# Rounding the encoder's angles on ScalarE instead of VectorE, in the first layer of a graph network

## The reference

```
rel_t     = node_vec[src] - edge_weight                        # one number per edge
rel_t_enc = cos(rel_t[:, None] * time_w + time_b)              # 32 numbers per edge
e         = concat([rel_t_enc, edge_attr_64]) @ We             # 96 -> 128
k, v      = (x @ Wk + bk)[src] + e, (x @ Wv + bv)[src] + e
alpha     = sum(q[dst] * k, per head) / 8
out       = segment_softmax(alpha, dst) weighted sum of v, by dst
x         = layernorm(x + out + x @ Wskip + bskip)
```

## Time and profile before

| | |
|---|---|
| median of 3 runs | 12685.32 us (12684.47 to 12685.91) |
| time of the profiled execution | 12758.32 us |
| its span | 12756.5 us |
| first and last gather of the first layer (L560) | 226.0 us and 6285.6 us |
| PE, DVE, ACT, POOL busy from 300 to 6000 us | 4130.52, 4032.91, 2634.28, 3696.79 us |
| the same from 6400 to 12756 us | 3715.91, 2565.70, 1396.91, 5152.92 us |

### The profile page before, as it was taken

How to read it: one execution, slowest core, us unless ns; L and a number is a source line. 1 busy time by engine, 2 the same in 40 slices (tenths; PEclk the granted TensorE clock), 3 DMA queues, 4 the chain that set the end, 5 groups by cost and what they waited for, 6 DMA issues and landing times.

```text
span 12756.5 us, 215589 instructions
## 1 busy us (share of the span) xinstructions
PE 8280.4 (65%) x44603; PEld 7400.1 (58%) x44604; DVE 7035.3 (55%) x23935; ACT 4268.4 (33%) x14084; POOL 9104.8 (71%) x7644
## 2 busy tenths in 40 slices
PE   5777777777777777777645555555555555555555
PEld 2666666666666666666635555555555555555555
DVE  4776776777777777767763333333333333333334
ACT  1444444444444444444422222222222222222221
POOL 2666666666666666666468888888888888888884
PEclk8777877787777777777766666666666666666667
DMA  6555555555555555555533333333333333333335
GB/s 184 150 149 146 148 149 149 148 152 148 150 148 148 150 152 150 148 149 149 135 37 35 35 35 35 35 35 35 35 35 35 35 35 35 35 35 35 35 35 120
DMA packets 1699357, 1205.64 MB, mean 95 GB/s; under 512 B 749995, under 2 KB 1471983, under 8 KB 1699023
## 3 DMA queue, kind: packets, MB, share of 16 engines
q0 software_dynamic: 634368, 675.42, 32.8%
q1 hardware_dynamic: 1013840, 503.68, 15.2%
q10 hardware_dynamic: 51072, 25.69, 0.7%
HBM read 924.83 MB, written 279.22 MB: 94 GB/s over the span
## 4 chain that ended last, share of the span: by engine, by line
DMA 22%; issue 20%; POOL 19%; DVE 13%; another core or an unknown queue 9%; PE 8%; DVEq 4%; SPq 3%; ACT 2%; POOLq 0%; ACTq 0%
DMA part_scratch<-kve,idx 21%; POOL part_scratch L609 19%; DVE y_all L1142 3%; PE bank L703 2%; DVE acc L1275 2%; PE bank L694 1%; DVEq L375 1%; PE bank L684 1%; DVEq L273 1%; PE bank L676 1%; DVE ohT L1135 1%; ACT wv L859 1%; DVE oh L1188 1%; DVE oh L1181 1%
## 5 line engine op out<-in xcount | busy, mean ns | idle before, releaser
L609 POOL DMA_INDIRECT part_scratch<-kve,idx x3232 | 5134.7, 1589 | 1056.8 <-issue 884.2
L560 POOL DMA_INDIRECT kv<-kv_scratch,took x3520 | 3544.5, 1007 | 2303.4 <-issue 1366.8
L761 PE MATMUL bank<-ident,kv 128*128 128x128 f32 x3232 | 753.4, 377 | 2403.8 <-DVE ohT L1364 2314.6
L1390 DVE TENSOR_TENSOR idx<-kv,twins 128x4 int32<-128x4 f32 x808 | 131.4, 163 | 3627.2 <-DMA part_scratch<-kve,idx 3627.2
L761 PEld LDWEIGHTS bank<-ident,kv 128*128 128x128 f32 x3232 | 489.4, 188 | 2582.1 <-ACT kv L940 2217.7
L859 ACT ACTIVATE wv<-tables,weights 128x65 f32<-128x65 f32 x7040 | 1771.5, 337 | 3.5 <-PE bank L703 2.5
L771 PE MATMUL bank<-ohT,oh 128*128 128x128 f32 x6464 | 1644.2, 435 | 148.6 <-DVE oh L1356 138.8
L771 PEld LDWEIGHTS bank<-ohT,oh 128*128 128x128 f32 x6464 | 1408.1, 321 | 423.7 <-DVE oh L1356 357.0
L947 ACT ACTIVATE oh<-bank 128x512 f32<-128x512 f32 x808 | 482.4, 597 | 3258.4 <-PE bank L771 3258.3
L703 PE MATMUL bank<-wv,oh 128*128 128x130 f32 x7040 | 1302.3, 342 | 363.4 <-issue 239.3
L1123 DVE TENSOR_TENSOR tables<-kv,bank 128x512 f32<-128x512 f32 x880 | 599.7, 681 | 1682.1 <-remote 1610.8
(11 more groups left out here) (166 smaller groups left out, 9952.4 us busy)
## 6 DMA issues: line engine op xcount, KB each, us to landing
kve<-nodes_scratch SPq DMA_DIRECT2D x880, 256.0 KB
feat<-in_edge_attr_dram SPq DMA_DIRECT2D x880, 96.0 KB
kv<-kv_scratch,took POOLq DMA_INDIRECT x3520
qb<-q_scratch SPq DMA_DIRECT2D x880, 64.0 KB
part_scratch<-kve,idx POOLq DMA_INDIRECT x3232
part_scratch<-zrow SPq DMA_DIRECT2D x220, 128.0 KB
feat<-in_edge_attr_dram SPq DMA_DIRECT2D x880, 32.0 KB
kv<-part_scratch ACTq DMA_DIRECT2D x56, 448.0 KB, 6.0
```

The lines of the kernel that those rows point to most:

```text
L560: pool.indirect_dma_start(kv[:, k, g, :], None, kv_d, bass.IndirectOffsetOnAxis(ap=took[:, j, g, 0:1].bitcast(I32), axis=0)).then_inc(s_ga ...
L609: pool.indirect_dma_start(part_d[g], bass.IndirectOffsetOnAxis(ap=idx[:, k, g:g + 1], axis=0), sum_ring[:, k, g, :], None, compute_op=ALU. ...
L761: op = pe.transpose(banks[0][:, g * P:(g + 1) * P], taken[:, st.k, 0, g:g + 1].to_broadcast([P, P]), ident[:, :])
```

## The change

DVE's `angle(1)` goes away. A new stage on ACT, `turn_stage`, adds MAGIC as the bias of an Identity activation, with the bias in a column `magic` of one element per partition, and signals `s_turn`. It stands directly ahead of `sine_stage` on ACT and waits for DVE's `angle(0)`. What was `angle(2)` is now `angle(1)`; it waits for `s_turn` and stands on DVE behind `ke_stage`. `ANG`, the number of angle steps on DVE for a batch, is 2 instead of 3. The column `magic` is set once at the start.

```diff
+        magic = sb("magic", [P, 1])
...
-        ANG = 3
+        ANG = 2
...
+            def turn_stage(st):
+                act.wait_ge(s_ang, ANG * st.batch() + 1)
+                act.activation(turns[:, :, :], encodings(st), ACT.Identity, bias=magic[:, :]).then_inc(s_turn, 1)
+
             def sine_stage(st):
                 act.wait_ge(s_ang, ANG * (st.batch() + 1))
...
-                    sines = [(sine_stage, 16)] if k % BATCH == 0 else []
+                    sines = [(turn_stage, 16), (sine_stage, 16)] if k % BATCH == 0 else []
...
+            dve.memset(magic[:, :], MAGIC)
...
+                    if n == 1:
+                        dve.wait_ge(s_turn, st.batch() + 1)
                     if n == 0:
                         op = dve.tensor_tensor(a, a, brow[:, :].unsqueeze(1).to_broadcast([P, BATCH * G, TD]), ALU.add)
-                    elif n == 1:
-                        wait(dve, s_ang, done)
-                        op = dve.tensor_scalar(t, a, MAGIC, None, ALU.add)
                     else:
                         op = dve.scalar_tensor_tensor(out=a, in0=t, scalar=MAGIC, in1=a, op0=ALU.subtract, op1=ALU.subtract)
...
-                    at(i, k, *turn[0], (ve_stage, 14), *turn[1], (ke_stage, 14), *turn[2], (block_stage, 0), *once(5, forward_stage),
+                    at(i, k, *turn[0], (ve_stage, 14), (ke_stage, 14), *turn[1], (block_stage, 0), *once(5, forward_stage),
```

More of the change, by code:

```diff
@@ L237, in build @@
         s_oh, s_oht, s_rel0, s_pen, s_gap = sem("s_oh"), sem("s_oht"), sem("s_rel0"), sem("s_pen"), sem("s_gap")
+        s_turn = sem("s_turn")
         s_rel, s_arg, s_ang, s_enc, s_feat, s_featc = sem("s_rel"), sem("s_arg"), sem("s_ang"), sem("s_enc"), sem("s_feat"), sem("s_featc")
```

## The result

| | before | after |
|---|---|---|
| median of 4 runs each | 12685.61 us (12684.47 to 12686.27) | 12915.60 us (12907.28 to 12924.54) |
| time of the profiled execution | 12758.32 us | 12924.54 us |
| its span | 12756.5 us | 12922.7 us |

The changed kernel takes 1.0182 times as long (95% interval 1.0164 to 1.0199): slower by 230 us, where 55 were forecast, and outside the range. The profiled executions differ by only 166 us, since the one of before lay 73 us above its median and the one of after 9 us above its own.

A forecast was written before the change was run, and what follows sets the result against it. No engine was full; a loop of POOL's eight gathers and angle multiplication, then DVE's odd-step additions, bounds it. Per round 0.4 + 0.3 - 0.2 = 0.5 us, times 110 = +55 us: about 12740 us, range 12640 to 12870.

The forecast's parts named there:

- the mechanism of the wait, and the side: DVE's last angle step waits for ACT's turn, partly covered by idleness: slower, 0.42 as likeliest case, 0.58 for slower overall.
- ACT's own price: ACT, 440 added Identity activations over 128x256 with a bias column: 0.50 us each, ends 0.34 and 0.71.
- table load ahead of the turn: Rival: ACT's sine table loads before the turn, so DVE waits for it too: 141 us more, 12865 us, chance 0.08.
- iteration 388: Even iteration with the running maxima, no DVE idleness: last step 1.9 us late, carried to the odd L1128, cost 0.4 us.
- Added wait: DVE's last angle step waits for ACT's turn behind its copies, priced over four even iterations a round: 0.4 + 0.3 us.
- the 0.2 us a round saved: Removing L1114 from DVE brings the even L1128 0.2 us earlier, counting in one batch in four: 0.2 us a round.
- the 73 us carried over: The profiled execution stood 73 us above the median; the same difference was taken from 12813 us to give about 12740.
- Iteration 390: Even iteration behind the round's exponentials, ACT late: 5.2 us late against 4.60 idle, 0 one round later; mean 0.3 us.
- Hidden altogether: Rival: DVE's 3.8 us of idleness a batch takes in all the added waits: 12685 us, chance 0.20.
- Faster by the even L1128: Rival: L1128 of the even step 0.2 us earlier, where POOL's fifth gather is due: 12620 us, chance 0.15.
- The held ACT: Rival: PE's late signals hold ACT's copies and now DVE, one batch in eight, 3 us each: 12850 us, chance 0.15.

## Why the prediction was wrong

**Right: the mechanism of the wait, and the side.** DVE's last step stands behind ACT's scaled copies, everything behind it on DVE is late, and part of that is covered by idleness ahead of the odd addition to v. The forecast idleness of about 2 us a batch was measured as 2.1, the fall at the addition as 535 us against a wait of 601. Taking the hand-over out from behind the copies, or the waiting step to the end of the list, gives back 172 and 183 of 230 us. Two of its signs came otherwise: the period of a batch is 14.2 us, not 13.9, and in iterations like 388 the odd addition to v came 0.82 us later after the even one on average, not 2.

**Right: ACT's own price.** The turn takes 495 ns against the 0.50 taken, and ACT's extra work alone is worth 1.0004 on both levels.

**Right: no table load ahead of the turn.** The changed kernel's ACT, in order of time, behind a round's exponentials:

```profile
3016.89 0.50 ACT L872 ACTIVATE turns<-feat,magic 128x256 f32<-128x256 f32 x1
3017.41 1.28 ACT L878 ACT_TABLE_LOAD   x1
3018.70 0.51 ACT L878 ACTIVATE feat<-feat,zero 128x256 f32<-128x256 f32 x1
```

The Identity ran under the exponential's table and the load came behind it, so this rival's 141 us never arose. This agrees with the Trainium skill (ScalarE: Activation LUTs, Table sets: the hidden batching unit), by which a cheap function such as identity is in every set. The placement for the longest run of a block, in the Trainium skill (ScalarE activation tables: per-element evaluation and per-set limits, Table sets in the compiler and the runtime), I had read as beginning the sine's run at the turn; in this trace the exponential's run goes on through the turn, so that reading did not hold here.

**Wrong: the cost of iteration 388 under "Added wait", sized at 0.4 us a round.** This is the step that failed first. I carried the 1.9 us to the odd L1128 and to POOL, found POOL late by only 0.4, and stopped. Behind the same DVE step stand the running maxima, and PE, in order, stands behind these with its transposes, then the features' transposes and the next edge projection. So the delay reached the addition to v of the next even step, where POOL waits too. The prediction even noted that DVE has no idleness in this iteration, and followed one of the two who wait for it. Measured in the two traces: +2.43 us behind the maxima and +0.82 ahead of them, less 1.58 given back two steps on, against +0.4; and by experiment the one late turn of k mod 8 = 4 is worth 1.27 - 0.48 = 0.79% of 12690, 100 us or 0.9 us a round. The term was also summed a little short: by its own rule the last step starts at 3046.11 + 0.6 = 3046.7, not 3046.6, and the cost is near 0.6 us.

**Wrong in sign: the 0.2 us a round saved.** "L1114 delays L1128 by 0.2 us, so without it L1128 is earlier" is true of the instruction and false of the time. With the step away and nothing added, the kernel is 24 us slower on the remote level; on the POOL-bound one two kernels that differ only in whether a step stands between the two additions are 261 us apart. On the remote level, with the turn at the head of ACT's list and the last step between the additions, the ratio is 0.9910. Of these two edits the first adds nothing on the POOL-bound level (1.0163 and 1.0160), so I put the turn of sign down to the place; on the remote level the two weren't separated. With the turn ahead of the scaled copies 58 us of loss stay (12741.16 - 12682.94). The removal alone accounts for 24 of them; the other 34 weren't separated either, and 193.4 us of waiting ahead of the last step are still in that trace.

**The sum, as it should have been**, per round on the remote level:

| term | forecast | by the runs |
|---|---|---|
| late turn, k mod 8 = 4 | 0.4 us | 0.79% of 12690 / 110 = 0.9 us |
| late turn, the other three | 0.3 us | (1.34 - 0.79)% = 0.6 us |
| addition gone from DVE | -0.2 us | 24 / 110 = 0.2 us |
| what else stays with the turn early | none | (58 - 24) / 110 = 0.3 us, cause not shown |
| sum | 0.5 us | 2.0 us, against 230 / 110 = 2.1 |

That the sum comes out is no proof: the first two and the last two terms are parts of one measured difference.

**Wrong: the 73 us carried over.** I subtracted them from the forecast of the profiled execution; in the later runs the profiled execution lay within 20 us of its median. The execution that the durations came from was the unusual one. It did not move the forecast, which was the median plus 55 us either way, but the profiled one was expected at 12813 and came at 12924.54.

**Iteration 390** was forecast at 0.3 us a round. In the averages that place gave 1.58 us back after what had been lost two steps ahead of it, and on the POOL-bound level an early turn there alone gives back 183 us while the others are late. On the remote level it was not tried by itself.

**The rivals.** Hidden altogether: fell. Faster by the even L1128: fell, and its premise has the wrong sign. Table load: fell. The held ACT comes nearest in time, 12850, but the waits that grew are placed in one iteration of the round, not struck at random one batch in eight; it counts as part of the same wait, with the wrong rate.

**What stays open.** Why POOL's gathers last 1.00 or 1.09 us by what DVE does in the meantime: that the place of one DVE step sets it is shown, the mechanism is not; and that the same place helps on the remote level for the same reason is argued, not shown. Why PE's results reach DVE late on one level and not on the other is open too: it went with the chip, and no edit here changed it. The 34 us that stay with the turn early on the remote level have no cause shown.

## What to carry to other kernels

When a step on an in-order engine gets late, follow every engine that waits for anything behind it, not only the one that the loop is known by, and start with the once-a-round work, which had the least slack here. A hand-over to an idle engine is free only if that engine reaches it before its own waits: put the borrowed operation at the head of its list, and make its input an iteration earlier. That took the wait away here and still left 188 us of loss; the version that won also moved the waiting step to another place, and this place alone was worth 261 us. So try the places too. Cover that appears as "remote" idleness may be gone in the next execution of the same kernel: price the wait once with it and once without.

## What the runs showed of the hardware

One and the same kernel ran at 12683 to 12690 us in two groups of runs and at 11750 to 11751 us in three, by chip, with TensorE's mean granted clock in the two profiled executions at 0.727 and 0.748 of full speed. The difference is in the first layer: 1610.8 us of "remote" idleness ahead of DVE's addition to v in one trace, none in the other, and with it POOL's wait for k, 900.3 us or none. An indirect gather's issue on POOL, of one form and size, took 1.013 or 1.086 us on average according to where one 0.42 us step of DVE stood, which moved the whole program by 261 us. And POOL's subtraction of eight columns took 222 ns on average in the kernel before and 452 ns in the changed one on the POOL-bound level. An activation of 128x256 with a bias column took 495 ns as Identity and 508 ns as sine, and the sine started 1.29 us after the start of the table load ahead of it, which itself took 1.28 us.
